# Self-attention of a decoder layer: VectorE inverts the row sums and normalises the outputs straight from the two PSUM banks

## The chip, the core and the metric

The kernel runs on one core of a Trainium2 chip. The metric is the device time of one execution in microseconds (us). All numbers below are from three timed runs and one profiled execution of the kernel before.

## What is computed

One decoder layer on two sequences of 1024 rows with 512 features: a self-attention in a dilated window, a cross-attention over a context of 2048 rows, and a gated feed-forward part. Only the first is touched:

```python
def attn(x, qkv_w, qkv_b, out_w, out_b):            # x is layer-normalised before
    q, k, v = split(x @ qkv_w.T + qkv_b)            # 16 heads of 32
    q = q / (norm(q) + 1e-6);  k = k / (norm(k) + 1e-6)
    allowed = (abs(j - i) <= 16) & ((j - i) % 2 == 0)
    attn = softmax(where(allowed, q @ k.T, -inf))
    return (attn @ v) @ out_w.T + out_b
x = x + attn(layernorm(x)); x = x + xattn(layernorm(x), ctx); x = x + ffn(layernorm(x))
```

The softmax is done in two parts: the kernel sums exp(score) times v, and exp(score) alone, and divides the one by the other at the end.

## The kernel before

The even and odd rows of a sequence don't see each other, so the self-attention works on four **strips** (`s` = 0 to 3) of 512 rows. A strip has four groups of four heads and four tiles of 128 rows, hence 16 **units** (`n` = 0 to 15): unit n is tile `n % 4` of group `n // 4`. The code below writes out, for every engine, one loop over strips and units; each engine runs its own list strictly in order and waits on semaphores. In unit n TensorE does, in this order: the scores of unit n+1 (`scores`, L970), a slice of other work (projections of this or the next strip, transposes, the output projection and the query projection of the strip before), and `weighted(s, n)`: eight small matmuls of probabilities with v into `o_bank` (L984) and with ones into `r_bank` (L988), the last of which raises `pv_done`. ScalarE takes the exponent (L616), GpSimd multiplies with the band mask (L496), and the result is the next unit's probabilities.

There is one `o_bank` and one `r_bank` (PSUM, 512 columns each), and all four units of a group add into them. So before the first unit of the next group (n = 4, 8, 12, or 0 of the next strip) TensorE must wait until the group's results have left both banks. In the kernel before that wait is `o_copied` (L981): ScalarE copies the row sums into `rsum` (L624) and the outputs into `o_sc` (L625). Later VectorE inverts `rsum` in two halves in two different units (`inverse`, L809), GpSimd multiplies (`out_scale`, L505), ScalarE rounds to the upper half (`out_hi`, L630), GpSimd takes the rest (`out_lo`, L510, raises `ot_lo`), and the output projection reads both. `pieces` gives the whole 512 columns, and two halves only for the last group.

Everything else goes through a ring of four PSUM banks (`work`, `NR = 4`), handed out in the order that `uses()` writes. `take` makes TensorE wait until the bank's user four places earlier has been freed by ScalarE or VectorE. Two kinds of user matter here. `("len", s, p)` is a bank in which VectorE (`lengths`, L770 to L792) turns square sums of q and k into inverse lengths `rnrm`: a chain of 14 small instructions that sits in units 4 and 12. GpSimd multiplies q and k with `rnrm` (`scale_units`, L490), and only then can TensorE transpose them (`heads`, L953). `("kt", ...)` and `("qt", ...)` are these transposes, whose rest VectorE takes in `heads_lo` (L798, L802). VectorE's other work in a unit: `qk_tile` (L755), `square_sums` (L761), `turned` (L749), `residual` (L815), `constant` (L822, L826), and the layer-norm statistics. Strips 1 and 2 carry in units 4 to 15 the work of their two neighbours; strip 0 has no strip behind it and strip 3 none ahead.

Of the kernel before, what the change touches and what calls it, by code (L numbers as in the profile page):

```python
# [16 lines left out]
ALU = mybir.AluOpType  # L17
# [8 lines left out]
SEQ = 512  # L26
ST = SEQ // P
# [73 lines left out]
def attention_phase(nc, ctx, plan, sem, score, work, ident, mhalf, wait_pad, q_const,  # L101
# [175 lines left out]
    rsum = sb("rsum", [P, SEQ])  # L277
    o_sc = sb("o_sc", [P, SEQ])
# [18 lines left out]
    scb, o_bank, r_bank = score[:, 0:2, :], score[:, 2, :], score[:, 3, :]  # L297
# [86 lines left out]
    def group(s, g):  # L384
        return s * HG + g

    def pieces(k):
        half = SEQ // 2
        return (slice(0, half), slice(half, SEQ)) if k == NS * HG - 1 else (slice(0, SEQ),)
# [17 lines left out]
    pv_done = sem("pv_done")  # L407
    o_copied = sem("o_copied")
    rs_done = sem("rs_done")
    os_done = sem("os_done")  # L410
    ot_hi = sem("ot_hi")
    ot_lo = sem("ot_lo")
# [12 lines left out]
    with nc.Block() as block:  # L425
# [39 lines left out]
        def _(pool):  # L465
            PL = nc.gpsimd
# [32 lines left out]

            def out_scale(k):  # L500
                for n, c in enumerate(pieces(k)):
                    pool.wait_ge(rs_done, 2 * k + 2 if len(pieces(k)) == 1 else 2 * k + n + 1)
                    if n == 0:
                        pool.wait_ge(o_copied, 2 * k + 2)
                    PL.tensor_tensor(o_sc[:, c], o_sc[:, c], rsum[:, c], ALU.mult).then_inc(os_done, 1)  # L505

            def out_lo(k):
# [14 lines left out]
            for s in range(NS):  # L522
                more = s + 1 < NS
                for n in range(UN):
                    if n not in LATE:
                        mask(s, n + 1)
                    if n == 1 and s:
                        out_scale(group(s, -1))
                    if n == 2 and s:
                        out_lo(group(s, -1))  # L530
                    if n in (2, 3) and s:
                        out_bias(s - 1, 2 * n - 4)
                        out_bias(s - 1, 2 * n - 3)
                    if n in (5, 6):
                        scale_units(s, n - 3)
                    if n in (13, 14) and more:
                        scale_units(s + 1, n - 13)
                    if n in (2, 3, 4, 5) and more:
                        root1(s + 1, n - 2)
                    if n in (6, 9, 13):  # L540
                        out_scale(group(s, n // 4 - 1))
                    if n in (6, 7, 8, 9) and s:
                        root2(s - 1, n - 6)
                    if n == 7:
                        mask(s, 8)
                    if n in (7, 10, 14):
                        out_lo(group(s, {7: 0, 10: 1, 14: 2}[n]))
                    if n == 15 and more:
                        mask(s + 1, 0)
            s = NS - 1  # L550
            out_scale(group(s, 3))
            for t in range(ST):
# [6 lines left out]
        def _(act):  # L559
# [59 lines left out]

            def copy_out(k):  # L620
                act.wait_ge(pv_done, k * ST + ST)
                if k:
                    act.wait_ge(ot_lo, k)
                A.copy(rsum[:], r_bank).then_inc(o_copied, 1)  # L624
                A.copy(o_sc[:], o_bank).then_inc(o_copied, 1)  # L625

            def out_hi(k):
# [29 lines left out]
            for s in range(NS):  # L657
                more = s + 1 < NS
                for n in range(UN):
                    t = n % ST  # L660
                    if t == 0 and (s or n):
                        copy_out(group(s, n // 4 - 1))
                    if n not in LATE:
# [40 lines left out]
            s = NS - 1  # L704
            copy_out(group(s, 3))
            out_hi(group(s, 3))
# [12 lines left out]
        def _(dve):  # L719
# [85 lines left out]

            def inverse(k, half):
                c = slice(half * SEQ // 2, (half + 1) * SEQ // 2)
                dve.wait_ge(o_copied, 2 * k + 1)
                V.reciprocal(rsum[:, c], rsum[:, c]).then_inc(rs_done, 1)  # L809

# [37 lines left out]
            for s in range(NS):  # L848
                more = s + 1 < NS
                for n in range(UN):  # L850
                    t = n % ST
                    if n == 0:
                        heads_lo(s, 1)
                    if n == 6:
                        heads_lo(s, 2)
                    if n == 8:
                        heads_lo(s, 3)
                    if n == 14 and more:
                        heads_lo(s + 1, 0)
# [13 lines left out]
                    if n in (1, 2, 3, 5) and more:  # L873
                        spread1(s + 1, {1: 0, 2: 1, 3: 2, 5: 3}[n])
                    if n in (0, 1) and s:
                        inverse(group(s, -1), n)
                    if n in (5, 6):
                        inverse(group(s, 0), n - 5)
                    if n in (8, 9):
                        inverse(group(s, 1), n - 8)  # L880
                    if n in (12, 13):
                        inverse(group(s, 2), n - 12)
                    if n < 4:
# [9 lines left out]
            s = NS - 1  # L893
            inverse(group(s, 3), 0)
            inverse(group(s, 3), 1)
            for t in range(3):
# [11 lines left out]
        def _(pe):  # L908
# [65 lines left out]
            def weighted(s, n):  # L974
# [5 lines left out]
                if i == 0 and k:  # L980
                    pe.wait_ge(o_copied, 2 * k)  # L981
                for h in range(HPG):
# [953 lines left out]
```

## Time and profile before

| | us |
|---|---|
| time, median of 3 runs (lowest to highest) | 1314.2 (1312.85 to 1314.47) |
| the profiled execution: its own time | 1315.69 |
| its span, first to last instruction | 1314.0 |
| PE busy / DVE busy / ACT busy / POOL busy | 1238.7 / 555.7 / 418.2 / 234.5 |
| self-attention, first unit to the end of the last unit's row sums | about 79.6 to 391.6 |
| its tail (output and query projection of strip 3) | 391.6 to 443.8 |
| cross-attention and feed-forward part | the rest |

PE is TensorE, DVE VectorE, ACT ScalarE, POOL GpSimd, SP the engine that issues most DMAs. A row of the time order reads: start, duration, engine, line, operation, output<-inputs, shapes, count; in brackets how long the engine had been idle, and what ended it. An idle time whose end shows no semaphore is named "issue". The granted TensorE clock (PEclk) is a share of 2.4 GHz, so 0.50 is 1.2 GHz.

### The profile page before, as it was taken

Reading aid. Unit: us, or ns where it says so; the run is one execution under the profiler, and the core shown is the slowest. Engines: PE = TensorE matmul, PEld = TensorE weight load, DVE = VectorE, ACT = ScalarE, POOL = GpSimd, SP = SyncE. Lnnn points to the kernel's source line nnn. Section 1 sums busy time; section 2 is a strip of 40 time slices with the busy share of each in tenths; the row PEclk is TensorE's granted clock in tenths of the full one; section 3 lists DMA queues with packets and bytes.
Section 4 is the critical chain, followed back from the end, with each engine's and each line's share of the span. In section 5 each row is a group of like instructions: output and inputs, shape, how many; then the busy total and the mean of one; then the engine's idle time right before and its main releaser. Section 6 shows DMA issues by size and latency. Waiting matters only on the chain.

```text
span 1314.0 us, 17223 instructions
## 1 busy us (share of the span) xinstructions
PE 1238.7 (94%) x6888; PEld 997.0 (76%) x6888; DVE 555.7 (42%) x1046; ACT 418.2 (32%) x756; POOL 234.5 (18%) x230
## 2 busy tenths in 40 slices
PE   6899999999975789999999999999999999999999
PEld 4567777777754668888778888887788888888887
DVE  5446675675554263333346233325444223114112
ACT  4245445454341352222334222224332111111111
POOL 0146755654653000000000000000000000000000
PEclk9789999999987999999999999999999999999999
DMA  6100010101121452001143000031330000100000
GB/s 240 64 10 25 9 57 10 64 33 66 60 72 62 148 180 72 25 24 40 43 126 104 24 25 32 32 127 57 105 97 32 32 0 12 52 0 0 33 0 32
DMA packets 47812, 73.31 MB, mean 56 GB/s; under 512 B 4224, under 2 KB 16512, under 8 KB 47744
## 3 DMA queue, kind: packets, MB, share of 16 engines
q1 hardware_dynamic: 44480, 66.08, 15.2%
q10 hardware_dynamic: 3264, 6.29, 1.6%
q8 instruction: 47, 0.77, 0.2%
q14 instruction: 21, 0.17, 0.0%
HBM read 55.58 MB, written 16.78 MB: 55 GB/s over the span
## 4 chain that ended last, share of the span: by engine, by line
PE 57%; issue 4%; DVE 3%; ACT 1%; DMA 1%; POOL 0%; ACTq 0%; DVEq 0%; POOLq 0%
PE score L68 10%; PE score L66 10%; PE score L67 10%; PE work L66 8%; PE work L68 7%; PE work L67 7%; PE work L1500 2%; PE work L1472 1%; DVE cn_l L1350 1%; ACT x_pr L1275 0%; PE work L1509 0%; DMA x_stage<-in_ctx_n 0%; PE score L1822 0%; DVE fxn L1754 0%; DMA x_q_raw<-qp_scratch 0%
## 5 line engine op out<-in xcount | busy, mean ns | idle before, releaser
L66 PE MATMUL score<-fxt_h,w_hl 128*128 128x512 f32 x384 | 149.6, 389 | 0.8 <-DVE fxt_l L1759 0.8
L68 PE MATMUL score<-fxt_h,w_hl 128*128 128x512 f32 x384 | 149.4, 389 | 0.0
L67 PE MATMUL score<-fxt_l,w_hl 128*128 128x512 f32 x384 | 149.4, 389 | 0.0
L1779 DVE SCALAR_TENSOR_TENSOR hid<-score,gate 128x512 f32<-128x512 f32 x48 | 33.2, 692 | 236.6 <-ACT gate L1708 236.6
L1429 DVE TENSOR_TENSOR pt_l<-work,pt_h 128x512 fp32r<-128x512 f32 x64 | 44.0, 691 | 183.0 <-ACT pt_h L1315 182.9
L1708 ACT ACTIVATE gate<-score 128x512 f32<-128x512 f32 x48 | 28.7, 598 | 265.9 <-PE score L68 265.8
L66 PE MATMUL score<-ct_h,x_q_h 128*128 128x512 f32 x256 | 103.6, 405 | 2.6 <-ACT x_pr L1275 2.6
L496 POOL TENSOR_TENSOR probs<-probs,band 128x544 f32<-128x544 f32 (+1 forms) x64 | 89.5, 1398 | 75.2 <-ACT probs L616 75.0
L66 PE MATMUL work<-cn_h,pt_h 128*128 128x512 f32 x256 | 102.8, 402 | 0.0
L68 PE MATMUL score<-ct_h,x_q_l 128*128 128x512 f32 x256 | 100.9, 394 | 0.0
L67 PE MATMUL score<-ct_l,x_q_h 128*128 128x512 f32 x256 | 100.6, 393 | 0.0
L68 PE MATMUL work<-cn_h,pt_l 128*128 128x512 f32 x256 | 100.1, 391 | 0.0
L67 PE MATMUL work<-cn_l,pt_h 128*128 128x512 f32 x256 | 99.7, 389 | 0.0
L1247 POOL TENSOR_TENSOR xr<-xr,bv_row 128x512 f32<-128x512 f32 x16 | 20.8, 1301 | 436.3 <-DMA xr<-x_scratch 436.3
L66 PE MATMUL work<-wqkv_h,xt_h 128*128 128x512 f32 (+1 forms) x256 | 94.1, 368 | 2.4 <-DVE rnrm L792 2.0
L1315 ACT CAST pt_h<-work 128x512 fp32r<-128x512 f32 x64 | 37.2, 587 | 176.3 <-PE work L1500 176.3
L68 PE MATMUL work<-wqkv_h,xt_l 128*128 128x512 f32 (+1 forms) x256 | 88.0, 344 | 0.0
L67 PE MATMUL work<-wqkv_l,xt_h 128*128 128x512 f32 (+1 forms) x256 | 87.9, 343 | 0.0
L66 PEld LDWEIGHTS score<-fxt_h,w_hl 128*128 128x128 f32 x384 | 72.1, 188 | 16.0 <-issue 1.2
L67 PEld LDWEIGHTS score<-fxt_l,w_hl 128*128 128x128 f32 x384 | 72.1, 188 | 15.0
L68 PEld LDWEIGHTS score<-fxt_h,w_hl 128*128 128x128 f32 x384 | 72.1, 188 | 15.0
L66 PE MATMUL work<-w_hl,hid_h 128*128 128x512 f32 x192 | 75.6, 394 | 0.9 <-DVE xr L1387 0.8
(182 smaller groups left out, 2508.9 us busy)
## 6 DMA issues: line engine op xcount, KB each, us to landing
x_stage<-in_ctx_n SPq DMA_DIRECT2D x16, 512.0 KB, 4.2
x_stage<-in_ctx_n ACTq DMA_DIRECT2D x12, 512.0 KB, 3.6
x_in<-in_x SPq DMA_DIRECT2D x16, 256.0 KB, 2.6
xs<-in_x SPq DMA_DIRECT2D x4, 1024.0 KB, 5.2
x_scratch<-xs SPq DMA_DIRECT2D x4, 1024.0 KB, 4.7
qp_scratch<-xs SPq DMA_DIRECT2D x4, 1024.0 KB, 4.3
x_q_raw<-qp_scratch SPq DMA_DIRECT2D x16, 256.0 KB, 2.7
xr<-x_scratch SPq DMA_DIRECT2D x16, 256.0 KB, 2.6
```

The source lines that it names most:

```text
L66: pe.matmul(out, hi_s, hi_m, start=first, stop=False)
L67: pe.matmul(out, hi_s, lo_m, start=False, stop=False)
L68: return pe.matmul(out, lo_s, hi_m, start=False, stop=last)
L496: PL.tensor_tensor(probs[:, n % 2, :, 0:w], probs[:, n % 2, :, 0:w], band[:, c0:c0 + w].unsqueeze(1).to_broadcast([P, HPG, w]), ALU.mult). ...
L1247: nc.gpsimd.tensor_tensor(xr[:, par, :], xr[:, par, :], bv_row[:], ALU.add).then_inc(xb_done, 1)
L1315: nc.scalar.copy(pt_h[:, 4 * c:4 * c + 4, :], work[:, c % 2, :].rearrange("p (k q) -> p k q", q=P)).then_inc(pth_done, 1)
L1350: V.tensor_tensor(lo, stage[:, n % 4], hi.bitcast(F32), ALU.subtract).then_inc(nat_lo, 1)
L1429: V.tensor_tensor(pt_l[:, 4 * c:4 * c + 4, :], work[:, c % 2, :].rearrange("p (k q) -> p k q", q=P), pt_h[:, 4 * c:4 * c + 4, :].bitcast(F ...
L1472: last = PE.transpose(turn_bank(b, tile)[:, P * k:P * k + P], stage[:, n % 4, tile % 2, P * k:P * k + P], ident[:])
L1500: last = PE.transpose(work[:, c % 2, P * k:P * k + P], pr[:, 512 * c + P * k:512 * c + P * k + P], ident[:])
L1708: nc.scalar.activation(gate[:, f % 2, :], score[:, 2 * (f % 2), :], ACT.Silu, scale=WSCALE)\
L1779: V.scalar_tensor_tensor(hid[:], score[:, 2 * (f % 2) + 1, :], WSCALE, gate[:, f % 2, :], ALU.mult, ALU.mult).then_inc(hid_done, 1)
```

## The change

ScalarE's two copies, VectorE's two half inverses per group and GpSimd's product are gone. In their place VectorE runs `normalise(k)`: it waits for `pv_done` of the group's last unit, inverts the 512 row sums from `r_bank` into `rsum`, waits for `ot_lo` of the group before (which still reads `o_sc`) and for its own inverse, and multiplies `o_bank` with `rsum` into `o_sc`. TensorE waits for that product (`os_done`) where it waited for the copies. `normalise` stands at the start of units 0, 4 and 12, and in unit 8 behind `heads_lo(s, 3)`. The last group is multiplied in two halves, both behind both halves of the inverse.

```diff
-            def copy_out(k):                                   # ScalarE
-                act.wait_ge(pv_done, k * ST + ST)
-                if k:
-                    act.wait_ge(ot_lo, k)
-                A.copy(rsum[:], r_bank).then_inc(o_copied, 1)
-                A.copy(o_sc[:], o_bank).then_inc(o_copied, 1)
...
-            def out_scale(k):                                  # GpSimd, units 1 (of the next strip), 6, 9, 13
-                    PL.tensor_tensor(o_sc[:, c], o_sc[:, c], rsum[:, c], ALU.mult).then_inc(os_done, 1)
...
-            def inverse(k, half):                              # VectorE, units 0/1, 5/6, 8/9, 12/13
-                V.reciprocal(rsum[:, c], rsum[:, c]).then_inc(rs_done, 1)
+            def normalise(k):                                  # VectorE, units 0, 4, 8, 12
+                dve.wait_ge(pv_done, k * ST + ST)
+                parts = pieces(k)
+                for c in parts:
+                    V.reciprocal(rsum[:, c], r_bank[:, c]).then_inc(rs_done, 1)
+                if k:
+                    dve.wait_ge(ot_lo, k)
+                for n, c in enumerate(parts):
+                    dve.wait_ge(rs_done, k + n + 1)
+                    V.tensor_tensor(o_sc[:, c], o_bank[:, c], rsum[:, c], ALU.mult).then_inc(os_done, 1)
...
                 for n in range(UN):
                     t = n % ST
+                    if n in (4, 12) or n == 0 and s:
+                        normalise(group(s, n // 4 - 1))
                     if n == 0:
                         heads_lo(s, 1)
                     if n == 6:
                         heads_lo(s, 2)
                     if n == 8:
                         heads_lo(s, 3)
+                        normalise(group(s, 1))
...
                 if i == 0 and k:
-                    pe.wait_ge(o_copied, 2 * k)                # TensorE
+                    pe.wait_ge(os_done, k)
```

VectorE in strip 0 from the last square sums of unit 3 (L761) into the length chain of unit 4 (L770 onward), before:

```order
L761 TENSOR_REDUCE ss<-sq 128x16 [waits sq_done]
L770 TENSOR_SCALAR work<-ss 128x64 [waits ss_done,dve_freed]
L773 TENSOR_SCALAR work<-work 128x64 [waits newton_done]
L778 SCALAR_TENSOR_TENSOR ru<-work,ss 128x64 [waits newton_done]
L780 TENSOR_TENSOR ru<-ru,work 128x64 [waits newton_done]
```

The same place in the changed kernel (its lines L738 and L747 onward are the old L761 and L770 onward):

```order
L738 TENSOR_REDUCE ss<-sq 128x16 [waits sq_done]
L788 RECIPROCAL rsum<-score 128x512 [waits pv_done]
L793 TENSOR_TENSOR o_sc<-score,rsum 128x512 [waits rs_done]
L747 TENSOR_SCALAR work<-ss 128x64 [waits ss_done,dve_freed]
L750 TENSOR_SCALAR work<-work 128x64 [waits newton_done]
```

The inverse and the product now stand between the square sums and the length chain.

VectorE in strip 1 from the rest of the third group's q (L802, unit 8) to the first part of unit 9, before:

```order
L802 SCALAR_TENSOR_TENSOR qbd_l<-work,hmask,qbd_h 128x512
L755 TENSOR_TENSOR qk<-work,qkb_row 128x2x256 [waits filled]
L809 RECIPROCAL rsum<-rsum 128x256 [waits o_copied]
L761 TENSOR_REDUCE ss<-sq 128x16 [waits sq_done]
L749 TENSOR_TENSOR x2t_l<-work,x2t_h 128x4x128 [waits y_hi]
L822 SCALAR_TENSOR_TENSOR xn,cacc<-xn,wqb_row 128x512 [waits filled]
```

The same place in the changed kernel:

```order
L779 SCALAR_TENSOR_TENSOR qbd_l<-work,hmask,qbd_h 128x512
L788 RECIPROCAL rsum<-score 128x512 [waits pv_done]
L793 TENSOR_TENSOR o_sc<-score,rsum 128x512 [waits rs_done,ot_lo]
L732 TENSOR_TENSOR qk<-work,qkb_row 128x2x256 [waits filled]
L738 TENSOR_REDUCE ss<-sq 128x16 [waits sq_done]
L726 TENSOR_TENSOR x2t_l<-work,x2t_h 128x4x128 [waits y_hi]
```

Here the inverse moved ahead of `qk_tile`, directly behind `heads_lo`, as one instruction of 512 columns, and the product came behind it.

## Rows read from the trace of the kernel before

**Rows 1.** Two stretches: each engine's busy us (instructions), PEclk, DMA share, GB/s.
```profile
88.00:391.60 303.60, 289.76 (x2485) 221.74 (x2484) 195.85 (x400) 146.25 (x261) 182.35 (x163) 0.99 0.13 43
391.60:403.50 11.90, 0.00 (x0) 0.00 (x0) 3.36 (x2) 1.88 (x4) 7.54 (x9) 0.52 0.31 99
```
**Rows 2.** VectorE's groups, 60 to 445 us: busy us, mean ns | idle before.
```profile
L809 DVE RECIPROCAL rsum<-rsum 128x256 f32<-128x256 f32 x32 | 55.0, 1733 | 13.9 <-ACT rsum L624 13.8
...
L755 DVE TENSOR_TENSOR qk<-work,qkb_row 128x512 f32<-128x512 f32 x29 | 20.0, 690 | 36.7 <-PE work L68 36.7
```
**Rows 3.** Order of time, strip 0, around the start of unit 4's weighted sum.
```profile
93.97 0.68 DVE L761 TENSOR_REDUCE ss<-sq 128x16 f32<-128x512 f32 x1
...
95.50 0.44 PE L984 MATMUL score<-probs,v 128*32 128x136 f32 x8
...
98.13 0.56 DVE L792 RECIPROCAL rnrm<-work 128x64 f32<-128x64 f32 x1
...
99.60 1.91 POOL L490 TENSOR_TENSOR qk<-qk,rnrm 128x1024 f32<-128x1024 f32 x1
```
**Rows 4.** Order of time, strip 1, between the weighted sums of units 7 and 8.
```profile
186.28 0.41 PE L988 MATMUL score<-probs,ones 128*32 128x136 f32 x8
...
187.48 1.41 DVE L802 SCALAR_TENSOR_TENSOR qbd_l<-work,hmask,qbd_h 128x512 fp32r<-128x512 f32 x2 [0.48 <-ACT qbd_h L608]
...
190.64 0.44 PE L984 MATMUL score<-probs,v 128*32 128x136 f32 x8
```
**Rows 5.** Order of time, strip 0, units 11 to 14.
```profile
127.41 0.69 DVE L761 TENSOR_REDUCE ss<-sq 128x16 f32<-128x512 f32 x1 [0.70 <-ACT sq L595]
...
134.20 0.55 PE L953 MATMUL work<-ident,qk 128*128 128x128 f32 x3 [1.40 <-POOL qk L490]
```
**Rows 6.** Order of time, end of strip 0, unit 0 of strip 1.
```profile
141.27 0.41 PE L988 MATMUL score<-probs,ones 128*32 128x136 f32 x8
...
145.20 0.44 PE L984 MATMUL score<-probs,v 128*32 128x136 f32 x8
```
**Rows 7.** Order of time, strip 1, units 3 to 6.
```profile
159.53 0.68 DVE L761 TENSOR_REDUCE ss<-sq 128x16 f32<-128x512 f32 x1
...
163.69 0.56 DVE L792 RECIPROCAL rnrm<-work 128x64 f32<-128x64 f32 x1
...
164.63 0.44 PE L984 MATMUL score<-probs,v 128*32 128x136 f32 x8
...
165.83 0.38 PE L66 MATMUL work<-wqkv_h,xt_h 128*128 128x256 f32 x1
...
175.95 0.50 PE L66 MATMUL work<-wo_h,ot_h 128*128 128x512 f32 x1 [1.12 <-DVE kt_l L798]
```
**Rows 8.** Order of time, strip 1, units 11 to 13.
```profile
207.82 0.23 DVE L826 TENSOR_SCALAR q_const<-cacc,bqbk 128x4 f32<-128x4 f32 x1
...
210.29 0.44 PE L984 MATMUL score<-probs,v 128*32 128x136 f32 x8
...
213.01 0.40 PE L66 MATMUL work<-x2t_h,wp_h 128*128 128x512 f32 x1
```
**Rows 9.** Order of time, strip 3, units 4 and 5.
```profile
339.40 0.56 DVE L792 RECIPROCAL rnrm<-work 128x64 f32<-128x64 f32 x1
...
342.05 0.39 PE L66 MATMUL work<-wo_h,ot_h 128*128 128x512 f32 x1
```
**Rows 10.** Strip 3, units 8 to 11: two rows in time, one stretch.
```profile
362.61 0.44 PE L984 MATMUL score<-probs,v 128*32 128x136 f32 x8 [2.72 <-ACT o_sc L625]
...
371.42 0.95 PE L929 MATMUL work<-ident,xn 128*128 128x128 f32 x4 [2.01 <-ACT xn L574]
...
364.90:368.30 3.40, 3.40 (x33) 2.20 (x36) 3.32 (x10) 2.03 (x3) 2.68 (x4) 0.52 0.00 0
```
**Rows 11.** Order of time, the tail behind the last weighted sum.
```profile
397.81 4.92 POOL L515 TENSOR_TENSOR xs<-xs,ob_row 128x512 f32<-128x512 f32 x4 [0.93 <-DMA xs<-in_x]
...
403.56 0.76 PE L66 MATMUL work<-wo_h,ot_h 128*128 128x512 f32 x1 [11.96 <-POOL ot_l L510]
```

More of the change, by code:

```diff
@@ L407, in attention_phase @@
     pv_done = sem("pv_done")
-    o_copied = sem("o_copied")
     rs_done = sem("rs_done")
@@ L498, in mask @@
                                  ALU.mult).then_inc(p_ready, 1)
-            def out_scale(k):
[L501 to L504, printed above, removed]
-                    PL.tensor_tensor(o_sc[:, c], o_sc[:, c], rsum[:, c], ALU.mult).then_inc(os_done, 1)
             def out_lo(k):
@@ L526, in _ @@
                         mask(s, n + 1)
-                    if n == 1 and s:
-                        out_scale(group(s, -1))
                     if n == 2 and s:
@@ L539, in _ @@
                         root1(s + 1, n - 2)
-                    if n in (6, 9, 13):
-                        out_scale(group(s, n // 4 - 1))
                     if n in (6, 7, 8, 9) and s:
@@ L550, in _ @@
             s = NS - 1
-            out_scale(group(s, 3))
             for t in range(ST):
@@ L660, in _ @@
                     t = n % ST
-                    if t == 0 and (s or n):
-                        copy_out(group(s, n // 4 - 1))
                     if n not in LATE:
@@ L704, in _ @@
             s = NS - 1
-            copy_out(group(s, 3))
             out_hi(group(s, 3))
@@ L804, in heads_lo @@
                 last.then_inc(dve_freed, 1)
-            def inverse(k, half):
-                c = slice(half * SEQ // 2, (half + 1) * SEQ // 2)
-                dve.wait_ge(o_copied, 2 * k + 1)
-                V.reciprocal(rsum[:, c], rsum[:, c]).then_inc(rs_done, 1)
+            def normalise(k):
[8 more added lines that the diff above has]
+                    V.tensor_tensor(o_sc[:, c], o_bank[:, c], rsum[:, c], ALU.mult).then_inc(os_done, 1)
             def residual(s, t):
@@ L874, in _ @@
                         spread1(s + 1, {1: 0, 2: 1, 3: 2, 5: 3}[n])
[L875 to L882, printed above, removed]
                     if n < 4:
@@ L893, in _ @@
             s = NS - 1
-            inverse(group(s, 3), 0)
-            inverse(group(s, 3), 1)
+            normalise(group(s, 3))
             for t in range(3):
```

## The prediction, on record before the changed kernel ran

> **What bounds the kernel now.** I read the busy times by stretch first, then what TensorE waits for, then the order of time around each place where the two banks change hands. The stretches say that the self-attention's strips are TensorE's: from 88 to 391.6 us it is busy 289.8 of 303.6 us, VectorE 195.9, ScalarE 146.3, GpSimd 182.4 [rows 1]. What the change saves on ScalarE and GpSimd is time of engines with room. The question is therefore only how long TensorE now waits at the 15 places where a new group of heads takes `o_bank` and `r_bank`, and what is late because VectorE is held there. After them comes a tail in which TensorE idles 11.9 us [rows 1], looked at last.
>
> **What normalise costs.** The inverse of 256 row sums took 1.73 us, 32 times [rows 2]. The trace has no inverse of 512 columns from PSUM. Bounds: twice that row, 3.47, above; below, the inverse of 64 lengths, which does read PSUM, took 0.56 us [rows 3], so 192 more columns cost 1.73 - 0.56 = 1.17 us, 6.1 ns each, and 512 columns 0.56 + 448 x 0.0061 = 3.29 us. I take 3.36, between them. The product has one operand in PSUM and 512 columns like `qk_tile`: 0.69 us [rows 2]. With 0.05 us between the two, **VectorE is held 4.1 us per group**; from the last row-sum matmul to TensorE's restart it is 4.3 us with both handovers if VectorE is free, and longer by whatever VectorE still has to do. Before, the banks were free after ScalarE's two copies.
>
> The Trainium skill ("VectorE: DVE Perf Modes", section "First, the fixed hardware budget") says that the reciprocal is an iterated divide with a repeat count of 8. At the 0.96 GHz of that page's specifications 8 cycles a column would be an estimated 4.3 us for 512 columns, hence 0.9 us more per group and some 12 us more in all. The measured 6.1 ns a column is under 6 such cycles, so the row decides; what is left of that reading is rival 5. [...]
>
> **Place by place** (strip, unit). Times are those of before; "shift" is what all later work is moved by.
>
> - (0,4): VectorE finishes the square sums at 94.65, after the row sums are complete, so normalise runs 94.7 to 98.8, and the weighted sum starts at 98.95, not at 95.50 [rows 3]: 3.45 us late. The length chain stands behind normalise and so ends at 102.8, not 98.69. GpSimd, which began its product with the lengths at 99.60 [rows 3] because a mask held it, begins at 102.8, and TensorE's transposes wait for that product in both kernels. Shift **3.2**.
> - (0,8), (1,8), (2,8): in strip 1 the row sums end at 186.69, but normalise stands behind `heads_lo`, which ends at 188.89. It runs to 193.05, and TensorE starts at 193.2 instead of 190.64 [rows 4]. The other two places differ by hundredths. Shift **3 x 2.55 = 7.7**. VectorE's next steps are late by about as much as TensorE; with the old half inverses gone it has caught up by unit 10.
> - (0,12): VectorE is free at 128.10 [rows 5], and TensorE's next work but one, the transposes, again hangs on lengths and GpSimd's product: it already waits 1.40 us for them [rows 5]. The chain is 4.1 us longer; about 0.4 comes back since GpSimd's old product no longer stands ahead of the next mask. Shift **3.7**.
> - (1,0), (2,0), (3,0): VectorE is idle; the gap from the end of the row sums (141.68) to the weighted sum (145.20) is 3.52 us [rows 6], normalise needs 4.3. Shift **3 x 0.8 = 2.4**. `heads_lo(s, 1)` and `qk_tile` behind it come 4 us later, but the first is needed only at unit 4 and TensorE has two free banks.
> - (1,4), (2,4): VectorE is free at 160.21, normalise ends at 164.35, and TensorE wants the banks only at 164.63 [rows 7]. It is hidden there by the output projection. But the length chain moves from an end of 164.25 to 168.3, and its bank is the one that unit 5's projection takes, which started at 165.83 [rows 7]: 2.5 us late. Of this 1.1 comes back at unit 6, where TensorE waited 1.12 us for `heads_lo` [rows 7] behind a VectorE that no longer has two half inverses in units 5 and 6. Shift **2 x 1.35 = 2.7**.
> - (1,12), (2,12): VectorE was late, free only at 208.05 [rows 8]. In the changed kernel it is about 0.4 us less late, since the half inverses of unit 9 are gone: with the 2.55 us of unit 8 it is free at 210.2, normalise ends at 214.3 to 214.4 and the length chain at 218.35. Unit 13's query projection takes that bank; it started at 213.01 [rows 8], with the 2.55 at 215.56. Shift **2 x 2.8 = 5.6** (the weighted sum of unit 12, 210.29 before, is part of it).
> - (3,4): the same with less to hide it: the chain ends at 339.96 + 4.1, and the bank is that of the projection that started at 342.05 [rows 9]. Shift **2.0**.
> - (3,8): here TensorE already waits 2.72 us for the copy, and at unit 11 2.01 us for ScalarE's layer norm [rows 10]. That chain (transpose, upper half, rest, constant, norm) is what ends the stage; it starts without ScalarE's copies and without GpSimd's product ahead of the statistics. I get 2.6 us lost at unit 8 and all of it back by unit 11. Shift **0**. (3,12) is covered by four query projections: **0**.
>
> Sum: 3.2 + 7.7 + 3.7 + 2.4 + 2.7 + 5.6 + 2.0 = **27.3 us**. VectorE also does 16 products of 0.69 us more; where it isn't the one waited for, TensorE's work hides them, and they are in the 4.1 us elsewhere.
>
> **The tail.** The last group loses ScalarE's copies and GpSimd's products. Nothing is gained: GpSimd's four bias additions stand ahead of `out_lo`, start at 397.81 when a DMA has landed and take 4.92 us, and only then can the output projection start, at 403.56 [rows 11]. The DMA hangs on the query projection of strip 2, not on this group. **0**.
>
> **TensorE's clock.** Behind the waits of 2.72 and 2.01 us the granted clock fell to half (1.2 GHz): 0.52 over 3.4 us [rows 10], in which a fully busy TensorE does 1.7 us less work. The waits of 1.12 and 1.40 us had no such stretch behind them. Seven of the new waits are over 2.4 us, (0,4), (0,8), (0,12), (1,4), (1,8), (2,4), (2,8). Bounds: none falls, 0; all do, 7 x 1.7 = 11.9. These stages are denser than the one with the two falls, and some slow stretches would lie ahead of another wait. I take half, **6 us**.
>
> **Rivals.**
> 1. *No clock cost*: the stages are too busy for a fall. 1314.2 + 27.3 = 1341.5.
> 2. *The clock falls at every long wait*: 1314.2 + 27.3 + 11.9 = 1353.4.
> 3. *The delayed length chains are hidden* because VectorE and GpSimd, relieved later in the strip, catch up sooner than I step it. Then only the direct waits remain, 3.45 + 7.7 + 3.7 + 2.4 + two of 1.6 at unit 12 + about 1 at (3,4) = 21.4: 1335.6. Against it: the chain follows normalise at once, so nothing can be caught up in between.
> 4. *Not slower*: the inverse from the bank is as fast as a plain VectorE operation. With some 0.7 us for it, normalise would be 1.45 us, shorter than every gap; places (0,4) and (0,12) would still cost about 1 us each through the lengths, and the waits of 1.12 us (twice) and what the norm chain leaves of the 2.72 would go: about 1312 to 1314. It decides from an inverse under about 1.2 us. Against it: 0.56 us for 64 columns from PSUM [rows 3].
> 5. *A slower inverse from PSUM.* The 256-column row reads SBUF, and only the 64-column row reads PSUM. A quarter above their rate would be 0.85 us more at 14 places, 12 us: 1360. Against it: both rows together give one rate.
>
> I see no way in which the change would not do what it says, as VectorE's order holds both instructions at each place.
>
> **How the numbers follow.** The profiled execution took 1315.7 us (span 1314.0), the median is 1314.2; 33.3 us more is 1349.0 on the first and 1347.5 on the second. I put down 1348. Chances: the forecast 0.55, rival 1 0.18, rival 2 0.13, rival 3 0.07, rival 4 0.05, rival 5 0.02. The range 1333 to 1358 takes in the first four with the bounds of the inverse (15 x 0.1 us either way). Faster or slower means by over 0.2%, about what a measurement of this kernel can tell from none: faster 0.03, same 0.03 (both from rival 4 and errors of the same kind), slower 0.94.
>
> **What would show it.** The inverse at 3.3 to 3.5 us; ahead of L984's counterpart waits on the product of about 3.4, 2.5, 2.5 us in strips 0 to 2 and 0.8 us in unit 0; behind unit 4 waits for `rnrm`; 0.50 in PEclk behind some of them; the tail's idle time near 12 us; everything from 403.5 on unchanged but moved. The forecast fails if VectorE reaches normalise earlier than stepped, or if the waits in units 5 and 13 don't appear.

## The result, and the profile after

**The changed kernel took 1353.55 us (median of 4 runs, 1351.65 to 1354.69) against 1314.34 us (median of 4, 1312.85 to 1315.50): ratio 1.030 [1.028, 1.0315].** The prediction was 1348 us, between 1333 and 1358. It was right in direction and inside its range, and 5.5 us low. Rival 2, with the clock falling at every long wait, gave 1353.4; that it came so close is luck, as the table below shows.

The profiled execution is the fastest of the four (1351.65 us) and has a span of 1349.9 us, 35.9 more than before. First the page: the busy time of each engine, and TensorE's granted clock in 40 slices.

```profile
PE 1251.2 (93%) x6888; PEld 1008.5 (75%) x6888; DVE 566.6 (42%) x1048; ACT 402.1 (30%) x724; POOL 212.2 (16%) x213
...
PEclk9889998998998889999999999999999999999999
```

Second, the strips and the idle stretch behind them, as in [rows 1] (the columns are the same).

```profile
88.00:429.40 341.40, 302.68 (x2485) 232.53 (x2484) 205.26 (x400) 131.39 (x231) 161.60 (x148) 0.95 0.11 38
429.50:441.30 11.80, 0.00 (x0) 0.00 (x0) 3.93 (x4) 0.73 (x2) 5.97 (x7) 0.58 0.30 96
```

The same 2485 matmuls of the strips now stand in 341.4 us and not in 303.6. ScalarE is busy 14.9 us less there and GpSimd 20.8 us less, as the change promises, VectorE 9.4 us more. TensorE has 38.7 us without a matmul, 13.8 before, and its clock is 0.95, not 0.99. Third, what TensorE waited for from 70 to 480 us (total us, times, longest), and VectorE's two new groups (busy us, mean ns, idle before).

```profile
PE score L962 <- DVE o_sc L793: 28.7, 12, 5.2
PE work L66 <- POOL ot_l L502: 12.0, 1, 12.0
PE work L66 <- DVE rnrm L769: 5.4, 3, 2.3
```

```profile
L788 DVE RECIPROCAL rsum<-score 128x512 f32<-128x512 f32 (+1 forms) x17 | 53.6, 3160 | 32.1 <-PE score L966 32.0
...
L793 DVE TENSOR_TENSOR o_sc<-score,rsum 128x512 f32<-128x512 f32 (+1 forms) x17 | 11.1, 656 | 1.5
```

The weighted sum (now L962) waits 28.7 us for VectorE's product. Behind that come 5.4 us for `rnrm`, the inverse of the lengths, which stands behind normalise on VectorE. The tail's wait is the old one: 12.0 us, 11.96 in [rows 11].

Now the order of time. These rows are from the place of [rows 3], with unit 5's wait of strip 1 ([rows 7]) and unit 8's and unit 12's of the same strip ([rows 4], [rows 8]).

```profile
94.59 3.35 DVE L788 RECIPROCAL rsum<-score 128x512 f32<-128x512 f32 x1
...
97.97 0.69 DVE L793 TENSOR_TENSOR o_sc<-score,rsum 128x512 f32<-128x512 f32 x1
...
98.81 0.44 PE L962 MATMUL score<-probs,v 128*32 128x136 f32 x8 [3.23 <-DVE o_sc L793]
...
102.58 1.91 POOL L489 TENSOR_TENSOR qk<-qk,rnrm 128x1024 f32<-128x1024 f32 x1 [0.31 <-DVE rnrm L769]
...
179.61 0.39 PE L66 MATMUL work<-wqkv_h,xt_h 128*128 128x256 f32 x1 [2.25 <-DVE rnrm L769]
...
205.50 0.44 PE L962 MATMUL score<-probs,v 128*32 128x136 f32 x8 [2.38 <-DVE o_sc L793]
...
222.98 1.43 POOL L495 TENSOR_TENSOR probs<-probs,band 128x576 f32<-128x576 f32 x1 [2.08 <-ACT probs L603]
...
223.11 1.85 DVE L806 SCALAR_TENSOR_TENSOR xn<-xn,wqb_row 128x512 f32<-128x512 f32 x1
...
229.57 0.44 PE L962 MATMUL score<-probs,v 128*32 128x136 f32 x8 [3.04 <-DVE o_sc L793]
```

The inverse of 512 columns from PSUM takes 3.35 us and the product 0.69; the weighted sum starts at 98.81 (predicted 98.95), GpSimd's product with the lengths at 102.58 (predicted 102.8). The two traces can be laid over each other: the start of one and the same matmul after minus before is the delay up to there. At unit 4 of strip 0 it is 98.81 - 95.50 [rows 3] = 3.31 us, at unit 8 of strip 1 205.50 - 190.64 [rows 4] = 14.86, at the output projection behind the last strip 441.38 - 403.56 [rows 11] = 37.82. Taken from strip to strip and unit to unit in this way, the delay comes from:

| place (strip, unit) | predicted us | measured us | of it at half clock |
|---|---|---|---|
| (0,4) | 3.2 | 3.24 | |
| (0,8) | 2.55 | 4.02 | 1.56 |
| (0,12) | 3.7 | 3.33 | |
| (1,0), (2,0), (3,0) | 0.8 each | 0.85, 0.85, 0.84 | |
| (1,4) | 1.35 | 0.95 | |
| (1,8) | 2.55 | 3.95 | 1.48 |
| (1,12) | 2.8 | 4.42 | 1.48 |
| (2,4) | 1.35 | 2.48 | 1.55 |
| (2,8) | 2.55 | 3.88 | 1.40 |
| (2,12) | 2.8 | 5.83 | 2.88 |
| (3,4) | 2.0 | 1.94 | |
| (3,8) to (3,12) | 0 | 1.24 | |
| clock, not placed | 6 | | |
| sum to the output projection | 33.3 | 37.82 | 10.35 |

The last column is what a place lost between one matmul and a matmul of the next unit while TensorE hardly waited and the granted clock was at 1.2 GHz; at (2,4) it is the difference from (1,4). It is not all a price of the clock. At (1,12) and (2,12) the slower matmuls hid a wait for the length chain: in the run with filled waits (below), where the clock stayed up there, the same two places cost 4.09 and 4.08 us, of which 1.23 and 1.22 lie between units 12 and 13. By that run the clock's own part is about 0.3 us at (1,12) and 1.75 at (2,12), some 8.1 us in all and not 10.35, and the rest of the table is about 29.8 us.

Four such stretches, with the columns of [rows 1] (the last behind two falls):

```profile
120.50:124.50 4.00, 4.00 (x12) 3.05 (x11) 0.37 (x1) 0.50 (x1) 1.41 (x1) 0.57 0.02 4
206.00:209.40 3.40, 3.40 (x19) 2.56 (x12) 2.68 (x8) 2.34 (x4) 0.97 (x1) 0.50 0.02 5
277.50:281.50 4.00, 3.74 (x18) 3.70 (x19) 1.34 (x3) 0.45 (x2) 2.51 (x2) 0.57 0.00 0
328.50:336.00 7.50, 6.83 (x40) 5.74 (x41) 3.92 (x15) 1.02 (x2) 3.29 (x2) 0.54 0.01 3
```

TensorE is busy in them nearly throughout, and the clock is about half. Of the ten waits of 2.2 us or more for the product or for `rnrm` in the strips, nine have such a stretch beside them; the one of 2.25 us at 179.61 has none. A stretch doesn't always cost time: behind the waits of (0,4) and (0,12) the clock was 0.50 too (100.2 to 103.6 and 141.2 to 144.5), but there TensorE would have waited for the length chain next, and the delay that it had gathered by the next unit (4.28 us at unit 5) was back at 3.24 us by unit 6. Before, the strips had two such stretches, both in strip 3 ([rows 10] shows one).

The wait at unit 12 of strip 1, 3.04 us, is longer than the prediction stepped (about 1.6). VectorE came to normalise late because the last `constant` of unit 11 (L806) took 1.85 us beside GpSimd's mask. Before, it took 0.68 us and ended before the mask began:

```profile
207.09 0.68 DVE L822 SCALAR_TENSOR_TENSOR xn<-xn,wqb_row 128x512 f32<-128x512 f32 x1
...
207.94 1.43 POOL L496 TENSOR_TENSOR probs<-probs,band 128x576 f32<-128x576 f32 x1 [2.15 <-ACT probs L616]
```

With the delay of 16.33 us up to unit 11 taken off, the mask now starts 1.3 us earlier, since ScalarE has no copies to do ahead of the exponent. So relief of one engine brought two others together. Strip 2 shows the same at 322.57 and 322.70. This is read from the traces; no run took it away by itself.

The tail itself, as in [rows 11]:

```profile
435.64 4.92 POOL L507 TENSOR_TENSOR xs<-xs,ob_row 128x512 f32<-128x512 f32 x4 [5.83 <-DMA xs<-in_x]
440.52 1.41 POOL L502 TENSOR_TENSOR ot_l<-o_sc,ot_h 128x256 fp32r<-128x256 f32 x2
441.38 0.76 PE L66 MATMUL work<-wo_h,ot_h 128*128 128x512 f32 x1 [11.98 <-POOL ot_l L502]
```

Nothing is gained up to the output projection: TensorE idles 11.98 us. From 441.38 to the end of the span 1.9 us come back. About 1.0 of it is the clock: in the first 8 us of the output projection it was 0.65 before and is 0.78 now, because the half-clock stretch ends sooner after the start. The first row is of the kernel before, the second of the changed one.

```profile
403.60:411.60 8.00, 8.00 (x24) 6.33 (x25) 1.71 (x6) 0.00 (x0) 1.05 (x2) 0.65 0.01 2
```

```profile
441.40:449.40 8.00, 8.00 (x28) 6.37 (x29) 2.25 (x7) 0.48 (x1) 1.34 (x3) 0.78 0.01 2
```

### The profile page after: what moved, and what is told of

Same layout as the page of the kernel before. It is cut to its first block, busy times and chain, and to the rows that moved or that the text cites. A ratio compares the mean times of both kernels' runs of the same rounds, so it can differ in the third digit from the quotient of the medians.

```text
span 1349.9 us, 17161 instructions
## 1 busy us (share of the span) xinstructions
PE 1251.2 (93%) x6888; PEld 1008.5 (75%) x6888; DVE 566.6 (42%) x1048; ACT 402.1 (30%) x724; POOL 212.2 (16%) x213
## 3 DMA queue, kind: packets, MB, share of 16 engines
q1 hardware_dynamic: 44480, 66.08, 14.9%
## 4 chain that ended last, share of the span: by engine, by line
PE 56%; issue 4%; DVE 2%; ACT 1%; DMA 1%; POOL 0%; ACTq 0%; DVEq 0%; POOLq 0%
PE score L66 10%; PE score L68 10%; PE score L67 10%; PE work L66 7%; PE work L68 7%; PE work L67 7%; PE work L1478 2%; PE work L1450 1%; DVE cn_l L1328 1%; ACT x_pr L1253 0%; PE work L1487 0%; DMA x_stage<-in_ctx_n 0%; PE score L1800 0%; DVE fxn L1732 0%; DVE mx L1338 0%
## 5 line engine op out<-in xcount | busy, mean ns | idle before, releaser
L1686 ACT ACTIVATE gate<-score 128x512 f32<-128x512 f32 x48 | 28.7, 598 | 265.9 <-PE score L68 265.8
L66 PE MATMUL score<-ct_h,x_q_h 128*128 128x512 f32 x256 | 103.6, 405 | 2.6 <-ACT x_pr L1253 2.6
L66 PE MATMUL work<-wqkv_h,xt_h 128*128 128x512 f32 (+1 forms) x256 | 98.6, 385 | 6.9 <-DVE rnrm L769 6.5
L66 PE MATMUL work<-cn_h,pt_h 128*128 128x512 f32 x256 | 102.8, 402 | 0.0
L67 PE MATMUL work<-wqkv_l,xt_h 128*128 128x512 f32 (+1 forms) x256 | 92.0, 359 | 0.0
L68 PE MATMUL work<-wqkv_h,xt_l 128*128 128x512 f32 (+1 forms) x256 | 91.9, 359 | 0.0
L1225 POOL TENSOR_TENSOR xr<-xr,bv_row 128x512 f32<-128x512 f32 x16 | 20.8, 1297 | 435.3 <-DMA xr<-x_scratch 435.3
L68 PEld LDWEIGHTS score<-fxt_h,w_hl 128*128 128x128 f32 x384 | 72.1, 188 | 14.9
L67 PEld LDWEIGHTS score<-fxt_l,w_hl 128*128 128x128 f32 x384 | 72.1, 188 | 14.9
```

Source lines behind the costliest of these rows:

```text
L66: pe.matmul(out, hi_s, hi_m, start=first, stop=False)
L67: pe.matmul(out, hi_s, lo_m, start=False, stop=False)
L68: return pe.matmul(out, lo_s, hi_m, start=False, stop=last)
L1225: nc.gpsimd.tensor_tensor(xr[:, par, :], xr[:, par, :], bv_row[:], ALU.add).then_inc(xb_done, 1)
L1686: nc.scalar.activation(gate[:, f % 2, :], score[:, 2 * (f % 2), :], ACT.Silu, scale=WSCALE)\
```

## The experiments

The theory: TensorE waits because its two banks are held by VectorE for 4.1 us, mostly by the inverse, in a place of VectorE's order where other work stands ahead of it; and the length chain stands behind it. The first four runs separate the parts: the length of the hold, the bank's release, and the place in VectorE's order. Diffs are against the changed kernel unless a sentence says otherwise. The kernel before was measured again beside each group of runs (medians 1314.12 and 1314.98 us), and the ratios are against these; differences from the changed kernel are against its 1353.55 us.

### The hold made short

```diff
-                    V.reciprocal(rsum[:, c], r_bank[:, c]).then_inc(rs_done, 1)
+                    V.tensor_copy(rsum[:, c], r_bank[:, c]).then_inc(rs_done, 1)
```

> Leaves out the inverse: VectorE copies the row sums instead, so the outputs aren't normalised. Everything else, order and waits, is the changed kernel. Main theory (TensorE and the length chain wait for VectorE, which is held 4.1 us per group, 3.35 of them by the inverse): VectorE is held 1.4 us, shorter than nearly every gap. About 0.6 us stay at unit 4 of strip 0 and 1.0 at unit 12, 2.2 come back at the output projections of strips 1 and 2, 1 at strip 3: 1312 to 1314 us, no waits over 1.5 us for the product. Rival (the cost lies in the place of the work, in the handover between engines, or in VectorE reading the banks): at least half of the 39 us stay, 1334 or more.

Measured: 1313.95 us, ratio 0.9999 [0.9985, 1.0012]. What TensorE waited for, 70 to 500 us:

```profile
PE score L962 <- DVE o_sc L793: 4.8, 6, 2.5
```

This kernel leaves out the inverse, so its outputs are not normalised, but its instructions stand in the same order. It is as fast as expected. The wait for the product falls from 28.7 to 4.8 us and the loss is gone, so it hangs on how long the inverse keeps VectorE and the banks. The other half of the answer is as useful: even with an inverse that costs a copy, freeing ScalarE and GpSimd of their work gains nothing. (In its trace the last weighted sum of the strips starts at 389.26 and not at 390.92, but the median of ten runs shows no gain.)

### The banks freed early again, the rest as changed

ScalarE's two copies come back and release the banks; VectorE inverts and multiplies the copies, at the changed kernel's places in its order.

```diff
+            def copy_out(k):
+                act.wait_ge(pv_done, k * ST + ST)
+                if k:
+                    act.wait_ge(ot_lo, k)
+                A.copy(rsum[:], r_bank).then_inc(o_copied, 1)
+                A.copy(o_sc[:], o_bank).then_inc(o_copied, 1)
...
-                    V.reciprocal(rsum[:, c], r_bank[:, c]).then_inc(rs_done, 1)
+                    V.reciprocal(rsum[:, c], rsum[:, c]).then_inc(rs_done, 1)
...
-                    V.tensor_tensor(o_sc[:, c], o_bank[:, c], rsum[:, c], ALU.mult).then_inc(os_done, 1)
+                    V.tensor_tensor(o_sc[:, c], o_sc[:, c], rsum[:, c], ALU.mult).then_inc(os_done, 1)
...
-                    pe.wait_ge(os_done, k)
+                    pe.wait_ge(o_copied, 2 * k)
```

> ScalarE's two copies are back and TensorE waits for them, as in the kernel before; VectorE does inverse and product at the places of the changed kernel, from the copies in SBUF. Main theory: the direct waits (3.3, 2.4, 3.5, 0.8 us) vanish, but the length chains in units 4 and 12 stay 4.1 us late behind the inverse: 3.3 + 3.7 in strip 0, 1.4 + 2.8 in each of strips 1 and 2, 2.0 + 1.5 in strip 3, 19 us, and some 4 for the clock: about 1337 us (1331 to 1342). Rival (only the wait for the banks matters, the queue behind it is hidden): about 1318.

Measured: 1356.56 us, ratio 1.031 [1.0295, 1.033]. **The expectation of 1331 to 1342 failed**: early release alone gains nothing. The waits for the product are gone, and units 8 and 0 start on time, but what stood behind normalise got worse. The waits, 70 to 500 us:

```profile
PE work L66 <- DVE rnrm L780: 18.2, 5, 4.9
...
PE work L941 <- POOL qk L490: 5.8, 1, 5.8
...
PE work L917 <- DVE rnrm L780: 5.7, 1, 5.7
```

Waits for the length chain are 29.7 us, 5.4 in the changed kernel. The trace points to three reasons. The product, 17 times (ns: shortest, median, longest), and around two of its places:

```profile
L803 DVE TENSOR_TENSOR o_sc<-o_sc,rsum x17: 360/693/1823, 98.2 to 437.4; 128x512 f32<-128x512 f32 x15, 128x256 f32<-128x256 f32 x2
```

```profile
98.03 1.40 POOL L496 TENSOR_TENSOR probs<-probs,band 128x576 f32<-128x576 f32 x1
98.16 1.82 DVE L803 TENSOR_TENSOR o_sc<-o_sc,rsum 128x512 f32<-128x512 f32 x1
...
176.14 3.35 DVE L799 RECIPROCAL rsum<-rsum 128x512 f32<-128x512 f32 x1 [1.45 <-ACT rsum L612]
```

The product took 1.82 us instead of 0.69 where GpSimd's mask ran at the same time; six of the 15 took 1.26 to 1.82. The inverse now waits for ScalarE's copy, 1.45 us at this place, and a waiting VectorE holds the length chain too. And TensorE, no longer held at the banks, comes to the chain's end earlier and waits there in longer pieces: from 144 to 151.5 us the granted clock was 0.54. So the early release moved the wait from the banks to what stands behind normalise: mostly the chain, and in strips 1 and 2 also `x2t_l` behind unit 8, for which TensorE now waits 1.88 and 1.89 us. How much each reason costs isn't split by this run.

### The length chain put ahead of normalise

```diff
-                    if n in (4, 12) or n == 0 and s:
-                        normalise(group(s, n // 4 - 1))
+                    if n == 0 and s:
+                        normalise(group(s, -1))
...
+                    if n in (4, 12):
+                        normalise(group(s, n // 4 - 1))
```

The added lines stand behind `lengths`.

> The changed kernel with the length chain ahead of the inverse in units 4 and 12. Main theory: the chains are on time, but the banks come free 3.9 us later there: 6.1 + 5.9 us in strip 0, 2.85 + 5.65 in strips 1 and 2 each, 4.9 + 1.2 in strip 3, 7.5 at the units 8 and 2.5 at the units 0, 45 us without the clock and 55 to 60 with it: about 1372 us (1362 to 1380), slower than the changed kernel. Rival (the late length chain is the main cost): faster than the changed kernel, 1340 or less.

Measured: 1379.6 us, ratio 1.050 [1.048, 1.052]: at the upper edge of the expected 1362 to 1380.

```profile
PE score L964 <- DVE o_sc L793: 55.6, 14, 7.5
```

While the banks hang on VectorE, whatever stands ahead of normalise is added to the wait: 55.6 us, 28.7 in the changed kernel. Neither order of the two works: one delays the chain, the other the banks.

### Both: copies release the banks, and the lengths go first

The two edits above together.

> Both edits: ScalarE's copies free the banks, and the length chain stands ahead of inverse and product on VectorE. Main theory: neither wait is left. VectorE's hold now delays only the lower halves of x behind it in unit 4 (1.4 us in strip 0, 0.2 in strips 1 and 2) and the norm chain of strip 3 (1.5): about 1317 us (1313 to 1322). Rival (holding VectorE for 4.1 us in one piece, or taking GpSimd's product onto it, costs wherever it stands): 1330 or more.

Measured: 1326.34 us, ratio 1.0085 [1.007, 1.010]. Alone the edits cost 3.0 and 26.1 us over the changed kernel; together they save 27.2. Each opens the way for the other: with VectorE held as long as it is, most of the loss went only where VectorE neither releases the banks nor has the chain behind normalise. It missed its expectation of 1313 to 1322 by 4 us and is still 12 us over the kernel before. At unit 4 of strip 1 stands one wait that was counted at 0.2 us:

```profile
170.09 1.40 POOL L496 TENSOR_TENSOR probs<-probs,band 128x576 f32<-128x576 f32 x1
...
170.48 1.55 DVE L803 TENSOR_TENSOR o_sc<-o_sc,rsum 128x512 f32<-128x512 f32 x1
171.96 0.68 DVE L737 TENSOR_TENSOR xt_l<-work,xt_h 128x512 fp32r<-128x512 f32 x1
...
172.69 0.50 PE L66 MATMUL work<-wo_h,ot_h 128*128 128x512 f32 x1 [1.84 <-DVE xt_l L737]
```

The product is again stretched beside the mask, and now `xt_l`, next in VectorE's order, is what TensorE waits for, 1.84 us. Behind unit 8 of strips 1 and 2 it waits 1.88 us each for `x2t_l`, which wasn't counted at all. VectorE still does inverse and product in one piece of 4.0 to 5.8 us, and work that TensorE needs stands behind it.

### The same with the product back on GpSimd

Against "the banks freed early again": VectorE's product is removed and GpSimd's, with its old places, put back; VectorE keeps the inverse, in one piece, at the changed places.

```diff
+            def out_scale(k):
...
+                    PL.tensor_tensor(o_sc[:, c], o_sc[:, c], rsum[:, c], ALU.mult).then_inc(os_done, 1)
...
-                    V.tensor_tensor(o_sc[:, c], o_sc[:, c], rsum[:, c], ALU.mult).then_inc(os_done, 1)
```

> As the run in which ScalarE's copies free the banks (1356.6), with the product back on GpSimd, so that VectorE does only the inverse, in one instruction, at the place ahead of the length chain. Theory (that run was slow since the product took 1.26 to 1.82 us instead of 0.69 on VectorE wherever GpSimd's mask ran beside it, in front of the length chain): VectorE is held 3.35 us instead of 4.7 to 5.2; 1.8 us less at each unit 4, 0.7 to 1.3 less at units 12, and some half-clock stretches less: about 1343 us (1338 to 1348). Rival (the product's length doesn't matter, the inverse's late start does): 1352 or more.

Measured: 1337.89 us (1334.08 to 1341.65, a wider spread than the others), ratio 1.019 [1.016, 1.021], at the lower edge of the expected 1338 to 1348: 18.7 us less than with the product on VectorE.

```profile
PE work L66 <- DVE rnrm L792: 10.8, 5, 3.0
...
PE work L949 <- POOL qk L490: 4.4, 1, 4.4
PE work L925 <- DVE rnrm L792: 3.8, 1, 3.8
```

The waits for the chain fall from 29.7 to 19.0 us. In the profiled executions (this one is its kernel's fastest) the strips from 88 us on are 20.4 us shorter, 324.3 and 344.7 us. 16.1 us of it is time in which TensorE has no matmul (29.0 and 45.1 us), and 4.3 us is TensorE busy for less time with the same work, at a granted clock of 0.97 and not 0.96.

### Normalise ahead of `heads_lo` in unit 8

```diff
                     if n == 8:
-                        heads_lo(s, 3)
                         normalise(group(s, 1))
+                        heads_lo(s, 3)
```

> The changed kernel with inverse and product ahead of the third rest of q and k in unit 8 instead of behind it. Theory (the wait at unit 8 is 2.4 us because VectorE finishes heads_lo 2.2 us after the row sums): the wait shrinks to some 0.4 us in all four strips and the half-clock stretches behind it go; heads_lo has its banks free just in time for unit 9: about 1342 us (1339 to 1346). Rival (heads_lo's delay makes TensorE wait for its banks or for the scores instead): 1350 or more.

Measured: 1341.69 us, ratio 1.021 [1.019, 1.023], as expected, and 11.9 us less than the changed kernel. Unit 8 of strip 0, and the sum of the waits:

```profile
112.74 3.36 DVE L788 RECIPROCAL rsum<-score 128x512 f32<-128x512 f32 x1 [0.92 <-PE score L966]
116.21 0.69 DVE L793 TENSOR_TENSOR o_sc<-score,rsum 128x512 f32<-128x512 f32 x1
...
117.04 0.44 PE L962 MATMUL score<-probs,v 128*32 128x136 f32 x8 [0.79 <-DVE o_sc L793]
```

```profile
PE score L962 <- DVE o_sc L793: 20.5, 12, 3.5
```

VectorE is idle when the row sums end, and TensorE waits 0.79 us instead of 2.82. In strips 1 and 2 it waits 0.35 us; only in strip 3 are 3.18 us left of 5.22. This is the step of the prediction "normalise stands behind `heads_lo`": what `heads_lo` takes decides over these places. The product waits fall by 8.2 us and the time by 11.9; the difference of 3.7 fits the half-clock stretches of unit 8, which were 1.56 + 1.48 + 1.40 = 4.4 us in the table and are gone from the trace here.

### The waits filled with matmuls

Ahead of the wait for the banks in units 8 and 12, ten more matmuls of 512 columns go into the ring bank that comes next; their result is written over. TensorE has more to do, and the same wait.

```diff
+                if i == 0 and n in (8, 12):
+                    nxt = len(taken)
+                    wait_freed(pe, ring[nxt - NR])
+                    for j in range(FILL):
+                        PE.matmul(work[:, nxt % NR, :], wo_h[:, j % DK, 0:P], wp_h[:, j % DK, :],
+                                  start=True, stop=True)
```

> The changed kernel; in units 8 and 12 TensorE does ten extra 512-column matmuls (2.3 us at full clock, results overwritten) into the next free bank of the ring ahead of its wait for the product. Theory of the clock (of the 38 us in the strips some 9 are half-clock stretches of 3.4 us behind the waits of units 8 and 12): the waits stay as long but full, PEclk stays 1.00 there, 8 to 9 us less than the changed kernel: about 1345 us (1342 to 1348). Rival (the clock isn't set by these waits, or costs nothing): the same as the changed kernel, 1353, or slower by the extra work.

Measured: 1346.54 us, ratio 1.024 [1.023, 1.026], inside the expected 1342 to 1348: 7.0 us less than the changed kernel with 80 matmuls more. The same stretch behind unit 8 as above, and all strips:

```profile
120.50:124.50 4.00, 4.00 (x34) 2.89 (x34) 1.31 (x2) 0.94 (x2) 1.44 (x1) 1.00 0.01 4
88.00:430.00 342.00, 311.68 (x2548) 239.14 (x2544) 208.28 (x402) 132.04 (x233) 161.94 (x147) 0.97 0.12 42
```

The granted clock there is 1.00 instead of 0.57. Unit 8 of strip 0 adds as much delay as in the changed kernel (2.38 us against 2.47), but nothing more is added by unit 9 (0.01 us against 1.56). **So the half-clock stretches of unit 8 come from TensorE's idleness at the banks, and cost some 1.5 us each over the wait itself.** In unit 12 they cost less, since another wait comes out from under them once the clock stays up:

```profile
231.90 0.51 PE L66 MATMUL work<-x2t_h,wp_h 128*128 128x512 f32 x1 [0.96 <-DVE rnrm L770]
```

This is the query projection of unit 13, which waits for the length chain. In the changed kernel it didn't wait, because the matmuls ahead of it ran at 1.2 GHz until the chain had ended.

Not every fall is gone: the clock in the strips is 0.97, not 0.99. In unit 8 of strip 3 the ten matmuls didn't fill the wait, 2.82 us were left of it, and the clock fell beside it. Of the two waits of 2.28 us for `rnrm` in unit 5, the one of strip 1 (178.18) now has a fall beside it and the one of strip 2 (275.98) none, the other way round than in the changed kernel.

### The tail: the rest of the last group ahead of the bias additions

This is the kernel before, with one call moved on GpSimd: `out_lo` of the last group now stands ahead of the four `out_bias` and not behind them. Nothing of the change is in it.

```diff
+            out_lo(group(s, 3))
...
-            out_lo(group(s, 3))
```

> The kernel before with one edit: for the last group GpSimd takes the lower half of the outputs before it adds the bias four times. Theory (the tail's 12 us of idle TensorE are set by the DMA and the four bias additions, not by inverse and product): the output projection starts 5 to 6 us earlier, about 1309 us (1307 to 1311). Rival (the tail's end hangs on the same DMA further down, in the residual and the store): 1313 to 1315.

Measured: 1310.48 us (10 runs), ratio 0.997 [0.9961, 0.998]: **4.5 us under the kernel before, and the fastest kernel here.** Its waits, and GpSimd at the tail:

```profile
PE work L66 <- POOL ot_l L510: 6.1, 1, 6.1
```

```profile
396.34 1.41 POOL L510 TENSOR_TENSOR ot_l<-o_sc,ot_h 128x256 fp32r<-128x256 f32 x2
397.71 4.98 POOL L515 TENSOR_TENSOR xs<-xs,ob_row 128x512 f32<-128x512 f32 x4
```

The output projection waits 6.1 us and not 12, and the four additions now run beside it. That shows why the change gained nothing in the tail: it shortened the work ahead of a DMA and four additions which the projection waited for anyway.

## Why the prediction was right, and where it was off

- **What normalise costs**: right. Predicted 3.36 and 0.69 us, measured 3.35 and 0.69. The reading of 8 cycles a column (rival 5) and a fast inverse (rival 4) are both out.
- **Most places are set by VectorE's order**: right. Outside units 12 of strips 1 and 2, and without the half-clock part, the table sums to 21.6 us against 21.7 predicted, and no place is off by more than 0.42 except (3,8). The run with the short hold shows that the hold is the cause, the one with normalise ahead of `heads_lo` shows the 2.55 us of unit 8, and the run with both edits shows that the delayed chains count in their own right. Rival 3 is out: the waits for `rnrm` are there, and nothing was caught up between. Rival 4's time for a fast inverse, 1312 to 1314, is what the run with the short hold then took.
- **(1,12), (2,12), the mis-sized term**: predicted 2 x 2.8 = 5.6 us, measured 4.42 + 5.83 = 10.25. That is 4.65 us too little, and the whole sum was 4.5 us too small (33.3 against 37.82). The step that failed is "it is about 0.4 us less late": with the delay up to unit 11 taken off, VectorE came to normalise at 208.94 and not at 207.65, because the last `constant` was stretched from 0.68 to 1.85 us beside a mask that comes earlier without ScalarE's copies. The wait at unit 12 was 3.0 us and not 1.6, and the one for the chain at unit 13 came on top, as stepped (1.2 us). With the clock up the two places cost 4.1 us each. The rest, 0.3 and 1.75 us, is the clock, which fell here although these waits were not among the seven counted; in strip 2 it fell for twice as long.
- **(1,4), (2,4)**: predicted 1.35, measured 0.95 and, without the clock, 0.93; more of the chain's delay was taken back by unit 6 (2.33 us late at unit 5 of strip 1, as against 2.5, and 1.39 taken back, not 1.1).
- **(3,8)**: predicted 0, measured 1.24. TensorE lost 2.49 us at unit 8 as stepped (2.6), and 0.7 more by unit 9 at half clock; by unit 11, 2.0 of it came back and not all. The step "all of it back by unit 11" was too kind.
- **The clock**: the 6 us were met by luck. Half of the upper bound of 11.9 was a choice and not a reading. Of the seven waits that it counted, four cost 1.56, 1.48, 1.55 and 1.40 us, together 5.99; beside two, (0,4) and (0,12), the clock fell and it cost nothing; beside (1,4) it didn't fall. Rival 1 is out by these four. Rival 2, "at every long wait", isn't what happened either: its 11.9 us came near the total only because the two units 12 made up for it.
- **The tail**: right at 0 for the wait (11.98 us against 11.96). "Everything from 403.5 on unchanged but moved" was not quite so: 1.9 us came back there in the profiled execution, about half of it by the clock.
- **The gain the change was after**: 14.9 us of ScalarE and 20.8 us of GpSimd were saved in the strips, and worth nothing, as read from [rows 1]. The first experiment shows it directly.

## What to carry to other kernels

When an engine that works its list in order releases a buffer that another engine waits for, the price is the time it holds the buffer, plus what stands ahead of it, plus the delay of what stands behind it; all three are to be read off the order of time, and moving the release elsewhere may only move the wait. Work taken off engines that nobody waits for was worth nothing here; look first at which engine the bound one waits for. It can even cost: what such an engine does next comes earlier, and here it met VectorE. A long wait of TensorE inside dense work can be dearer than its length, since the clock is down for a stretch beside it. At four places that was about 1.5 us; where TensorE would have waited again anyway, it was nothing.

## What the runs showed of the hardware

- A product on VectorE with both operands in SBUF took 1.26 to 1.82 us in the run with copies, and 0.83 to 2.40 us in the run with both edits, instead of 0.69, at the places where a GpSimd operation ran at the same time. With one operand in PSUM it did not. This is the changed kernel's product beside a mask:

```profile
373.78 1.42 POOL L495 TENSOR_TENSOR probs<-probs,band 128x576 f32<-128x576 f32 x1
373.93 0.69 DVE L793 TENSOR_TENSOR o_sc<-score,rsum 128x512 f32<-128x512 f32 x1
```

  The inverse, with one operand, stayed at 3.29 to 3.36 us, from SBUF or PSUM. The Trainium skill, "SBUF — State Buffer", section "Who interferes with whom", says that a VectorE instruction with two SBUF inputs contends with a GpSimd instruction that reads SBUF, and that one with at most one SBUF input does not, outside the modes that use two ports. The rows agree on both counts. That the 18.7 us between the two kernels with copies are all due to this isn't shown, since the other one has no product on VectorE at all. The changed kernel has the same stretching in `constant`, whose two operands are in SBUF: 1.85 and 1.86 us at 223.11 and 322.70, beside a mask, and 0.68 us at 207.85 and 213.86, where the mask began only during it. GpSimd's own instruction was stretched as well where it began beside VectorE's product: its product with the lengths took 2.36 us instead of 1.91 in units 4 of strips 1 and 2 of the run with both edits.
- The inverse of 512 columns costs 3.35 us from either memory, 6.5 ns a column, nearly five times the 0.69 us of a product of the same shape.
- Of ten waits between 2.2 and 5.3 us, nine had the clock at 1.2 GHz beside them; the tenth, 2.25 us, did not, while one of 2.28 us at 277.76 did. In the run with filled waits the same two places changed roles, so the length of a wait alone doesn't decide. What does was not tried.
